# A fused attention and feed-forward kernel: x1 moved to its blocks between partitions, weights centred on TensorE, x1's low halves ahead of VectorE's last counts

## The reference

```python
xn = layernorm(x)
Q, K, V = xn @ wq.T, xn @ wk.T, xn @ wv.T           # head size 64
energy  = K.T @ V                                   # per batch, 64x64
x1 = x + (Q @ energy) * sqrt(3/64) @ wo.T
h  = square(relu(layernorm(x1) @ W_fc.T))           # 1024 wide
y  = h @ W_proj.T
mem = 0; repeat 5 times:
    mem = 0.9*mem + y - (mem > 1); count += (mem > 1)
out = x1 + count / 5
```

## Time and profile before

| | us |
|---|---|
| median of 3 runs (482.1, 485.59, 485.45) | 485.45 |
| the profiled execution, its own time | 485.44 |
| its span from the first to the last instruction | 483.4 |
| mean granted TensorE clock, share of full | 0.981 |

### The profile page before, as it was taken

The page is one execution under the profiler, slowest core; times in us unless marked ns, Lnnn a source line. Parts: engine busy times, 40 slices in busy tenths (PEclk is TensorE's granted clock), DMA queues, the critical chain, the costliest instruction groups (busy, mean ns, idle before and its releaser), DMA issues. The chain is left out here.

```text
span 483.4 us, 8236 instructions
## 1 busy us (share of the span) xinstructions
PE 459.1 (95%) x2856; PEld 409.2 (85%) x2856; DVE 364.7 (75%) x924; ACT 281.1 (58%) x519; POOL 237.9 (49%) x197
## 2 busy tenths in 40 slices
PE   7599899999999999999989999999999999999993
PEld 6478689898989889898979989898988889898993
DVE  4667648879887868878786888889787886758457
ACT  3338656756665755756665575766667475656530
POOL 1236635474655455564653556555554643444430
PEclk9989989999999999999998999999999999999998
DMA  8510304262352424253341424425142404130011
GB/s 300 123 45 25 64 0 133 43 171 50 87 132 66 126 72 130 45 154 64 79 128 57 130 45 113 106 77 130 57 96 44 125 1 103 45 90 38 34 45 43
DMA packets 120969, 41.29 MB, mean 85 GB/s; under 512 B 114016, under 2 KB 114656, under 8 KB 120672
## 3 DMA queue, kind: packets, MB, share of 16 engines
q1 hardware_dynamic: 120928, 40.78, 32.9%
HBM read 25.03 MB, written 15.73 MB: 84 GB/s over the span
## 5 line engine op out<-in xcount | busy, mean ns | idle before, releaser
L389 POOL TENSOR_TENSOR hid_l<-hid,hid_h 128x512 fp32r<-128x512 f32 x128 | 166.7, 1303 | 201.7 <-ACT hid_h L444 201.6
L431 ACT ACTIVATE relu<-hid_ps 128x512 f32<-128x512 f32 x128 | 76.5, 598 | 125.9 <-PE hid_ps L893 124.7
L892 PE MATMUL y_ps<-wdn_l,hid_h 128*128 128x256 f32 x480 | 136.6, 285 | 0.0
L893 PE MATMUL y_ps<-wdn_h,hid_l 128*128 128x256 f32 x480 | 136.5, 284 | 0.0
L891 PE MATMUL y_ps<-wdn_h,hid_h 128*128 128x256 f32 x480 | 136.1, 284 | 0.0
L891 PE MATMUL hid_ps<-x2T_h,wup_h 128*128 128x512 f32 x256 | 106.1, 415 | 5.5 <-DVE x2T_l L701 5.5
L892 PE MATMUL hid_ps<-x2T_l,wup_h 128*128 128x512 f32 x256 | 101.2, 395 | 0.0
L893 PE MATMUL hid_ps<-x2T_h,wup_l 128*128 128x512 f32 x256 | 100.5, 393 | 0.0
L770 DVE SCALAR_TENSOR_TENSOR cnt<-y_ps,bound,cnt 128x256 f32<-128x256 f32 x240 | 98.2, 471 | 0.2
L891 PEld LDWEIGHTS y_ps<-wdn_h,hid_h 128*128 128x128 f32 x480 | 92.5, 193 | 5.2
L892 PEld LDWEIGHTS y_ps<-wdn_l,hid_h 128*128 128x128 f32 x480 | 92.4, 193 | 4.9
(11 more groups left out here) (135 smaller groups left out, 577.3 us busy)
## 6 DMA issues: line engine op xcount, KB each, us to landing
xs<-x_dram SPq DMA_DIRECT2D x15, 512.0 KB, 4.6
out_dram<-x SPq DMA_DIRECT2D x15, 512.0 KB, 2.6
x_blocks<-x SPq DMA_DIRECT2D x56, 128.0 KB, 2.7
x_block<-x_blocks SPq DMA_DIRECT2D x14, 512.0 KB, 3.6
x_block<-x_dram SPq DMA_DIRECT2D x104, 64.0 KB, 2.6
hid<-w_up_dram SPq DMA_DIRECT2D x1, 1024.0 KB, 7.1
x<-w_down_dram SPq DMA_DIRECT2D x1, 1024.0 KB, 9.2
xs<-x_dram SPq DMA_DIRECT2D x2, 256.0 KB, 2.9
```

Source lines behind the costliest of these rows:

```text
L389: nc.gpsimd.tensor_tensor(hid_l[:, i % 2, c, :], hid[:, c % 4, :], hid_h[:, i % 2, c, :].bitcast(f32), ALU.subtract).then_inc(hid_ready, 1)
L431: nc.scalar.activation(relu[:, c % 2, :], hid_ps[c % 2][:, :], ACT.Relu).then_inc(relu_done, 1)
L892: mm(dst, a[0], b[1], start=False, stop=False)
L893: return mm(dst, a[1], b[0], start=False, stop=stop)
```

## The change

1. `scatter_x1` no longer goes through memory: 16 transfers per group, each from 32 partitions of x1 to 32 partitions of `x_block`, 8 runs of 128 bytes per partition. `gather_x1` and its wait are gone; `turn_x1` waits for all 16.
2. In VectorE's step `x2T_low_half` stands ahead of the last six operations of the first pair of counts, and `turn_blocks` behind `q_low_half` and `energy_sum`.
3. Weights are centred by TensorE alone: it multiplies by `centre` (identity minus 1/256) and `minus_mean` (-1/256), so that the centred weights appear in PSUM. W_fc is done in four blocks of 512 columns (`centre_up`), two products each. ScalarE rounds and VectorE takes the rest straight from PSUM; GpSimd no longer does W_fc.
4. The orders of the setup and of step 0 are new on all engines: second half of W_proj rounded inside step 0, K and V of group 3 projected earlier, moments of x1's group 1 behind K and V of group 3, fewer `keep_warm` rounds.

```diff
+        def small_centred(which):
+
+            return (y_ps[0], e_ps)[which][:, 0:2 * EC * HEAD].rearrange("p (k n) -> p k n", k=EC)
+
+        def up_block(b):
+
+            return (hid_ps[0], hid_ps[1], kv_ps, e_ps)[b][:, :]
+
+        def up_columns(b):
+
+            return b % EC, slice(b // EC * HID // 2, (b // EC + 1) * HID // 2)
...
             def scatter_x1(n):
                 sp.wait_ge(x1_ready, n + 1)
-                if n >= 4:
-                    sp.wait_ge(x1_blocks_back, 16 * (n - 3))
+                sp.wait_ge(x_turn, min(n, GROUPS - BY_MATMUL))
                 for b in range(4):
                     src = x1[32 * b:32 * (b + 1), n % RING, :].rearrange("q (s i e) -> q s i e", s=TILES * EC, i=4)
-                    sp.dma_start(x1_blocks[n % 2, :, :, :, b, :].rearrange("i q s e -> q s i e"), src)\
-                        .then_inc(x1_blocks_written, 16)
-
-            def gather_x1(n):
-
-                sp.wait_ge(x1_blocks_written, 64 * (n - 1))
-                sp.wait_ge(x_turn, min(n, GROUPS - BY_MATMUL))
-                sp.dma_start(x_block[:, :], x1_blocks[n % 2].rearrange("i q s b e -> (i q) (s b e)"))\
-                    .then_inc(x1_blocks_back, 16)
+                    for i in range(4):
+                        dst = x_block[32 * i:32 * (i + 1), :].rearrange("q (s b e) -> q s b e", s=TILES * EC, b=4)
+                        sp.dma_start(dst[:, :, b, :], src[:, :, i, :]).then_inc(x1_blocks_in, 16)
...
+            pool.wait_ge(ident_ready, 1)
+            pool.wait_ge(minus_mean_ready, 1)
+            nc.gpsimd.tensor_tensor(centre[:, :], ident[:, :], minus_mean[:, :], ALU.add).then_inc(centre_ready, 1)
...
-                    if c == (1 if is_first(r, i) else 4) and there(r, i + 3):
-                        inverse_deviation(r, 2 if is_first(r, i) else i + 3)
+                    if c == 4 and there(r, i + 3) and not is_first(r, i):
+                        inverse_deviation(r, i + 3)
...
-                if i == 0 and c == 1:
-                    act.wait_ge(wup_ready, 2)
...
+            def high_half_of_up(b):
+
+                act.wait_ge(wup_centred, b + 1)
+                k, cols = up_columns(b)
+                nc.scalar.activation(wup_h[:, k, cols], up_block(b), ACT.Copy).then_inc(wup_high, 1)
...
                         xT_high_half(0, 2)
                         xT_high_half(0, 3)
+                    if c == 1:
+                        half_of_columns(w_loaded["down"], wdn_raw, wdn_h, wdn_high, 1)
                     if c == 5:
                         x2T_high_half(0, 1)
-                    if c == 6:
                         kvT_out(0, 3)
...
             high_half_of_up(0)
             kv_high_half(0, 1)
+            q_high_half(0, 0)
+            energy_first_half(0, PER_BATCH - 1)
             q_high_half(0, 1)
-            energy_first_half(0, PER_BATCH - 1)
-            half_of_columns(w_loaded["down"], wdn_raw, wdn_h, wdn_high, 0)
             eo_high_half(0, PER_BATCH - 1)
             high_half_of_up(1)
-            half_of_columns(w_loaded["down"], wdn_raw, wdn_h, wdn_high, 1)
+            half_of_columns(w_loaded["down"], wdn_raw, wdn_h, wdn_high, 0)
+            high_half_of_up(2)
+            high_half_of_up(3)
             x2T_high_half(0, 0)
...
+            def low_half_of_up(b):
+
+                dve.wait_ge(wup_high, b + 1)
+                k, cols = up_columns(b)
+                nc.vector.tensor_tensor(wup_l[:, k, cols], up_block(b), as_f32(wup_h[:, k, cols]), ALU.subtract).then_inc(wup_ready, 1)
...
-                dve.wait_ge(x1_blocks_back, 16 * (n - 1))
+                dve.wait_ge(x1_blocks_in, 256 * (n - 1))
...
                 kv_scale(0, 2)
                 kv_low_half(0, 2)
+                first_moments(0, 3)
                 x2T_low_half(0, 1)
-                first_moments(0, 3)
-                moments(0, 1)
                 kv_scale(0, 3)
                 kv_low_half(0, 3)
+                moments(0, 1)
...
                 if there(r, i - 2):
                     spikes(r, i - 2, 1, range(0, PAIR_OPS // 2))
-                if there(r, i + 3):
-                    turn_blocks(i + 3)
                 if there(r, i + 2):
                     q_low_half(r, i + 2)
                 if there(r, i + 2) and closes_batch(i + 2):
                     energy_sum(r, i + 2)
+                if there(r, i + 3):
+                    turn_blocks(i + 3)
                 if there(r, i - 2):
...
                 if there(r, i + 1) and not x1_by_matmul(i + 1):
                     turn_x1(i + 1)
+                if there(r, i + 1):
+                    x2T_low_half(r, i + 1)
                 if there(r, i - 1):
                     spikes(r, i - 1, 0, range(PAIR_OPS // 2, PAIR_OPS))
-                if there(r, i + 1):
-                    x2T_low_half(r, i + 1)
-
-
-            centre_weights(w_loaded["kv"], wkv_raw[:, :], 0, wkv_centred)
-            centre_weights(w_loaded["qq"], wqq_raw[:, :], 1, wq_centred)
+
+
             first_moments(0, 0)
-            low_half_of_weights(wkv_high, wkv_raw[:, :], wkv_h, wkv_l, wkv_ready)
+            low_half_of_kv()
             xT_low_half(0, 0)
-            dve.wait_ge(wq_high, 1)
-            nc.vector.tensor_tensor(wq_hl[:, :, 1, :], wqq_raw.rearrange("p (k s n) -> p k s n", k=EC, s=2)[:, :, 0, :], as_f32(wq_hl[:, :, 0, :]),
-                                    ALU.subtract).then_inc(wq_ready, 1)
             xT_low_half(0, 1)
+            low_half_of_q()
             first_moments(0, 1)
             kv_scale(0, 0)
-            centre_up(0, 0)
             kv_low_half(0, 0)
             kv_scale(0, 1)
-            centre_up(0, 1)
+            low_half_of_up(0)
             kv_low_half(0, 1)
             q_low_half(0, 0)
             energy_sum(0, PER_BATCH - 1)
             q_low_half(0, 1)
             eo_low_half(0, PER_BATCH - 1)
-            centre_up(1, 0)
-            centre_up(1, 1)
+            low_half_of_up(1)
             residual(0, 0)
             x2T_low_half(0, 0)
+            low_half_of_up(2)
+            low_half_of_up(3)
...
+            def centre_weights(loaded, raw, which, done):
                 pe.wait_ge(loaded, 16)
+                w = raw.rearrange("p (k n) -> p k n", k=EC)
                 for k in range(EC):
-                    last = mm((y_ps[0], e_ps)[first][:, 0:2 * HEAD], averager[:, :], raw[:, k * 2 * HEAD:(k + 1) * 2 * HEAD],
-                              start=(k == 0), stop=(k == EC - 1))
-                last.then_inc(mean_done, 1)
+                    for j in range(EC):
+                        last = mm(small_centred(which)[:, k, :], (centre if j == k else minus_mean)[:, :], w[:, j, :],
...
+            def centre_up(b, part):
+                k, cols = up_columns(b)
                 rows = wup_raw.rearrange("p (k n) -> p k n", k=EC)
+                if part == 0:
+                    pe.wait_ge(w_loaded["up"], 16)
+                    if b < 2:
+                        pe.wait_ge(xT_ready, 2)
+                    elif b == 2:
+                        pe.wait_ge(kv_in_scale, 1)
+                    else:
+                        pe.wait_ge(eo_ready, 1)
+                done = mm(up_block(b), (centre if part == k else minus_mean)[:, :], rows[:, part, cols],
+                          start=(part == 0), stop=(part == EC - 1))
+                if part == EC - 1:
+                    done.then_inc(wup_centred, 1)
...
+                if n == 2:
+                    pe.wait_ge(wup_ready, 3)
...
-                    pe.wait_ge(wup_ready, 1 + 2 * c // FC)
+                    pe.wait_ge(wup_ready, 2 + 4 * c // FC)
...
                         turn_x1(1)
+                    if c == 5:
+                        project_kv(0, 3)
                     if c == 6:
                         energy_sum(0, 2)
-                        project_kv(0, 3)
-                    if c == 7:
                         turn_kv(0, 3)
...
             turn_first(0, 0)
             turn_first(0, 1)
-            keep_warm(3)
+            keep_warm(2)
             project_kv(0, 0)
-            project_q(0, 0)
+            centre_up(0, 0)
             turn_kv(0, 0)
             project_kv(0, 1)
-            average_up(0)
-            project_q(0, 1)
+            centre_up(0, 1)
             turn_kv(0, 1)
             energy_sum(0, 0)
+            project_q(0, 0)
+            centre_up(1, 0)
             energy_sum(0, 1)
-            keep_warm(2)
+            project_q(0, 1)
             energy_times_wo(0, PER_BATCH - 1)
-            average_up(1)
+            centre_up(1, 1)
+            centre_up(2, 0)
             attend(0, 0)
-            keep_warm(4)
+            centre_up(2, 1)
+            centre_up(3, 0)
+            centre_up(3, 1)
             turn_x1(0)
             keep_warm(3, work_ps[1])
```

More of the change, by code:

```diff
@@ L572, in _ @@
             kv_high_half(0, 0)
-            q_high_half(0, 0)
             kvT_out(0, 1)
@@ L593, in _, with low_half_of_kv, low_half_of_q @@
```

(42 more changed lines are left out.)

55 lines of the change are left out of this document (20 added, 35 removed).

## The result

The changed kernel takes 499.44 us (median of 4 runs, 498.14 to 501.08), the kernel before beside it 485.29: a ratio of 1.031, interval 1.026 to 1.036, so 3.1% slower. The forecast was 480.5 with a range of 476 to 500; the time lies at the upper edge of that range, on the other side of the kernel before. What came is the prediction's first rival, "SP's issue time becomes the path", to which it gave 500 us and a chance of 0.26. That 500 is hit so closely is in part luck, as the account at the end shows.

A forecast was written before the change was run, and what follows sets the result against it. TensorE, busy 26.96 of a 27.10 us step, was taken as the bound, others mattering only where it waits; 485.4 - 7.0 - 0.8 + 2.4 + 2.4 - 1.7 = 480.7, taken as 480.5, range 476 to 500.

The forecast's parts named there:

- first rival: SP's 16 issues at 0.67 each make x1 land 12.0 to 12.2 after ready: +20, so 500 us; chance 0.26.
- Part C: x1's 16 transfers on SP: landing 10.6 after x1 is ready, 2.2 us longer than before, which just fits.
- p: Distance of two transfer issues on SP, forecast 0.58 us between bounds of 0.37 and 0.69.
- D: Time from x1 ready to its blocks' landing, 15p + landing: forecast 10.6 us, bounds 7.5 and 13.
- D + 3.3: TensorE's start after x1 is ready: landing, then transpose, halves and handovers; due at 14.0, so landing up to 10.7 is free.
- a rival of 0.04: The clock falls at each step start, for up to 1.6 us more each: 505 to 520 us; chance 0.04.
- Groups 14 and 15: Shorter last steps without K and V work, TensorE due 12.4 after the scatter: +1.2 us each, +2.4 in all.
- Part A: The setup: step 0 starts at 29.0 instead of 36.03, -7.0 us, bounds -5 to -8.5.
- Part B: Steps 0 and 1: a stall and slow clock gained, new waits lost, -0.8 us, bounds +1 to -3.
- Part D: VectorE's reordering: `eo_l` later, attention waits 0.4 in six batch-closing steps, +2.4 us, bounds -5 to +5.
- The gain is eaten: Low halves end 0.3 earlier, but the count freeing `y_ps[0]` ends 1.62 later, so `project_down` starts again at 115.52.
- Step 8: Its 1.95 stall and slow clock make 3.5 us, laid to a late memory write; half taken, -1.7 us.

The follow-up runs named there:

- memory_way: The changed kernel with x1 going through memory again as before, new orders and new setup kept: 472.56 us, ratio 0.974 to the kernel before.
- low_last: The changed kernel with x1 through memory and its low halves behind all counts and sums, the blocks' turn where the change has it: 475.85 us, ratio 0.984.
- setup_only: The changed kernel with x1 through memory and VectorE's step order of before, so only setup and step 0 are new: 477.6 us, ratio 0.987.
- wide_sixteen: The changed kernel with 16 transfers of 256 bytes in each of 128 partitions, SBUF at both ends, x1's blocks wrongly arranged: 495.43 us.
- wide_out: The changed kernel with x1 through memory, written there by 16 transfers of 256 bytes in each of 128 partitions: 511.61 us.

## Why the prediction was wrong, point by point

- **Part C, p: this step failed.** The prediction took "the middle between 0.43 and 0.64", p = 0.58, on the ground that "the new transfer has half as many runs and one stride less at its source". p was 0.65 at best and 0.74 at worst, and D 11.7 to 13.0 instead of 10.6. Between two ends in SBUF, runs and strides are not what an issue is priced by: half the runs gave 0.64, unbroken ones 0.63, and what the rows of before could not show, both ends in SBUF, gives 0.60 an issue by itself. The first rival's ground ("both kinds of short-run issues take 0.64 to 0.69 though one has twice the runs") pointed the right way: the count of runs hardly mattered. The choice between two bounds was made by what seemed likely of the new shape, at a place where by its own sum each 0.01 of p beyond 0.59 costs 15 x 0.01 at 14 starts, some 2 us.
- **Part C, the rest: right.** The landing (1.95 forecast, 1.9), D + 3.3, and what is free: 10.7. With D at 4.0, and with 8.1 to 10.3, the time is the same; from 11.3 up it is 492 and more.
- **The first rival: right in its mechanism; its 500 us are right by luck in part.** "12 steps lose 1.4 + 0.1 each" and 1.5 at groups 14 and 15, +21 by these terms: the idles of the 12 steps are 0.84 to 2.15, 16.0 us in all, and 2.63 twice, together 21.3. But the clock, held apart as a rival of 0.04, came along with it, four falls of 1.7, so that the transfers cost 26.9 in the medians and 28.2 in the spans. What the rival left out there is made up for by the rest of the sum, which was 5.7 too high: 480.7 - 2.4 = 478.3 without the transfers' loss, where memory_way takes 472.6.
- **Groups 14 and 15.** D + 3.3 - 12.4 with the D that came gives 2.65; the row at 427.76 has 2.63. The term was +1.2 each only because D was too small.
- **Part A: right.** 29.59, and 28.99 in memory_way, against a forecast 29.0. Kernels with the same setup differ by up to 1.2 us there.
- **Part B: right within its bounds.** Steps 0 and 1 take 0.1 longer than before, with 1.64 of idle at step 2's start that belongs to the transfers; without it -1.5 where -0.8 stood. One of its terms didn't come: the 0.8 for GpSimd beside x's low halves. These take 1.29 us at 36.20 as elsewhere; it is GpSimd's W_proj operation, started at 37.11, that is stretched, to 2.66 (its first half took 2.36).
- **Part D: its mechanism was right, its sum wrong in sign.** "The gain is eaten": a plain step is 27.11 with the low halves last and 27.04 with them first, 0.07 of the 0.42 kept, and the row at 106.84 shows the wait for the bank that eats it. The late `eo_l` showed too, but only in 2 of the steps that close a batch, which are 0.9 longer, 1.9 in all where 2.4 stood. In one of them, on VectorE and GpSimd of memory_way:

```profile
161.14 1.85 DVE L777 SCALAR_TENSOR_TENSOR x<-cnt,x 128x256 f32<-128x256 f32 x2
```

```profile
161.19 1.51 POOL L377 TENSOR_TENSOR kv<-kv_scaled,kv 128x512 fp32r<-128x512 f32 x1
```

  The two sums took 1.85 us there, beside a GpSimd subtraction; in most steps 0.75. The first took 0.42 as elsewhere, the second 1.52, from 161.47 to 162.99, past the end of GpSimd's operation at 162.70. By the Trainium skill (SBUF — State Buffer, "Who interferes with whom") the engine that starts second waits for the whole of the other's operation, and the second sum does so here. In 9 of the 12 steps with this pair it is GpSimd's subtraction that is stretched instead, to between 1.85 and 1.87, though it starts before the second sum in them too; which of the two waits, the order of the starts alone doesn't tell.

  What the prediction had not seen lies elsewhere. From step 2 to step 13 low_last takes 301.2 us and memory_way 301.4: no difference. setup_only takes 302.5, with one late landing that the new order absorbs. Of the 4.4 between the spans of setup_only and memory_way (475.5, 471.1), 2.6 lie ahead of step 2 (0.4 of them in the setup, which is the same in both), 1.1 in those steps and 0.7 behind them. So the order was worth -5 and not +2.4, by the start, the end and the late landing, none of which stood in the sum.
- **Step 8.** The prediction laid its stall to "a late write to memory, which is gone". What made the write late is one stretched issue on SyncE, in the kernel before:

```profile
238.80 2.09 SPq L282 DMA_DIRECT2D x_blocks<-x  x1
```

  Such issues are not gone with the writes, for the changed kernel has them in 7 of its 14 batches. memory_way has one of 2.16 in the same batch; there the new order absorbs it, and no kernel of the memory way with the low halves ahead of the sums has an idle at step 8.

With the D of an undisturbed batch, 11.75, the prediction's own sum is 480.7 + 12 x 1.05 + 2 x 1.15 = 495.6. The stretched issues add 12 x 0.47 (mean D 12.2) and the four falls of the clock 6.8, which makes 508; the rest of the sum was some 6 too high, above all by the order, and that brings it back to about 502, where the profiled execution took 501.1. The sign was lost by one duration, p; the size has three errors in it, of which two add and one takes away.

## What to carry to other kernels

A chain of small transfers on one queue costs their issue times in a row, not their bytes. Before splitting a transfer, multiply the issue time by the count and compare it with the slack of whoever waits; if it doesn't fit, use a second queue, and if it does fit, nothing more is gained by a faster one. Where a forecast hangs on one unmeasured duration between two bounds, and the sign turns inside them, the bounds are the forecast. And look for an engine that waits for a partner ahead of work that needs no partner: moving the counts into that gap (468.6) gave more than the quickest way of x1 did (473.3).

## What the runs showed of the hardware

- An issue with both ends in SBUF takes 0.59 to 0.61 us on SyncE and 0.63 on ScalarE (medians; 0.52 for the first of a batch over 128 partitions), whether 16, 32 or 128 KB, 1, 4 or 8 runs, 32 or 128 partitions. With memory at one end the wide shape takes 0.33 as the first and 0.43 after another.
- Single issues are stretched to between 0.9 and 2.2 us, with either kind of end: in 7 of 14 batches of the changed kernel and in 2 of memory_way, which issues fewer transfers. The cause is open.
- What is issued right behind transfers with both ends in SBUF takes longer too: the load of x takes 0.59 to 0.60 there (104.23 in wide_sixteen) and 0.43 behind the others (104.49 in wide_out).
- ScalarE's arithmetic goes on beside its own issues: an activation at 93.02 between issues from 92.70 to 95.29.
- With both ends in SBUF, runs of 128 bytes land in 1.9 us and unbroken ones of 1 KB in 1.8.
- An idle of 1.83 us on TensorE was not followed by half the clock, one of 1.79 was. The length of the idle alone doesn't tell.
